# Attention with a maximum pass: the values matmuls of a full-width step in two halves, one unit of the maximum pass in between

## The reference, cut to what matters

```
q, k, v = heads(layernorm(x) @ W + b)            # 16 heads of 8
sim  = q @ k.T + bias(i - j) * SCALE             # relative position, bucketed
sim += where(j > i, -inf, 0)                     # causal
out  = softmax(sim) @ v                          # per head
x    = x + out @ Wo.T + bo
x    = x + layernorm(x + relu(t @ w1 + b1) @ w2 + b2) * gamma + beta    # t = layernorm(x)
```

## Time and profile before

| what | value |
|---|---|
| runs | 350.19, 349.46, 346.96 us; median 349.46 |
| the profiled execution | 348.02 us, its span 346.2 us |
| busy in the span | PE 291.8, DVE 273.9, ACT 189.5, POOL 86.9 us |
| one group, where the groups repeat (one to five) | 29.2 us |
| PE, DVE, ACT busy in it | 26.36, 25.90, 18.89 us |

### The profile page before, as it was taken

The page is one execution under the profiler, slowest core; times in us unless marked ns, Lnnn a source line. Parts: engine busy times, 40 slices in busy tenths (PEclk is TensorE's granted clock), DMA queues, the critical chain, the costliest instruction groups (busy, mean ns, idle before and its releaser), DMA issues.

```text
span 346.2 us, 8324 instructions
## 1 busy us (share of the span) xinstructions
PE 291.8 (84%) x3233; PEld 130.6 (38%) x3235; DVE 273.9 (79%) x968; ACT 189.5 (55%) x262; POOL 86.9 (25%) x127
## 2 busy tenths in 40 slices
PE   7855687878999998898999889889899888999980
PEld 4421332222334234334334423433433343358650
DVE  5565275688889888888989888898899968748895
ACT  2332198305656756765674685585566568762330
POOL 2114999700220202022022011202200001425351
PEclk9995599756999999999999999999999999999996
DMA  7445502540110112022020113123211102000022
GB/s 213 125 126 151 127 0 65 156 139 1 56 56 3 36 23 56 2 54 56 3 57 29 41 27 78 55 34 75 66 22 24 23 4 42 8 0 17 0 62 61
DMA packets 16263, 18.80 MB, mean 54 GB/s; under 512 B 4480, under 2 KB 11776, under 8 KB 16096
## 3 DMA queue, kind: packets, MB, share of 16 engines
q1 hardware_dynamic: 13488, 12.56, 15.3%
q10 hardware_dynamic: 816, 2.96, 3.0%
q0 software_dynamic: 1920, 2.76, 2.7%
HBM read 11.81 MB, written 4.23 MB: 46 GB/s over the span
## 4 chain that ended last, share of the span: by engine, by line
PE 51%; DVE 19%; ACT 14%; issue 6%; POOL 4%; DMA 3%; SPq 1%; ACTq 1%; DVEq 0%; POOLq 0%
PE ps L1145 16%; PE ps L1101 13%; ACT PT L729 9%; PE ps L1133 7%; PE ps L1116 7%; DVE FM L865 6%; DVE junk L872 3%; ACT TT L687 2%; POOL XN L566 2%; PE ps L1178 2%; PE ps L1034 2%; DVE st L929 2%; DVE U L982 1%; PE ps L1087 1%; DMA table_s<-in_table 1%
## 5 line engine op out<-in xcount | busy, mean ns | idle before, releaser
L729 ACT ACTIVATE PT<-ps 128x1024 f32<-128x1024 f32 (+1 forms) x192 | 144.7, 813 | 93.6 <-PE ps L1133 82.1
L865 DVE TENSOR_REDUCE FM<-ps 128x1 f32<-128x512 f32 (+2 forms) x192 | 109.2, 617 | 14.5 <-PE ps L1101 14.0
L872 DVE CUSTOM_DVE_ANT_0 junk<-ps,NBH 128x256 bf16<-128x256 f32 (+1 forms) x256 | 90.3, 400 | 24.7 <-PE ps L1101 24.5
L1101 PE MATMUL ps<-KA,QA 56*128 56x256 bf16 (+3 forms) x544 | 96.9, 292 | 10.6 <-DVE FM L865 7.4
L1116 PE MATMUL ps<-QA,KA 58*128 58x512 bf16 (+3 forms) x384 | 78.0, 334 | 17.5 <-ACT PT L729 14.6
L1145 PE MATMUL ps<-PT,VG 128*16 128x512 f32 (+3 forms) x768 | 87.3, 500 | 0.1
L1101 PEld LDWEIGHTS ps<-KA,QA 56*128 56x128 bf16 x544 | 33.0, 96 | 97.2 <-DVE FM L865 40.6
L420 POOL DMA_DIRECT2D KA<-qk_scratch x24 | 12.9, 542 | 156.7 <-PE ps L1133 156.4
L1116 PEld LDWEIGHTS ps<-QA,KA 58*128 58x128 bf16 x384 | 25.0, 94 | 37.1 <-ACT PT L729 30.2
L1133 PE MATMUL ps<-TT,flb 128*32 128x176 f16 (+4 forms) x1152 | 38.7, 244 | 0.0
L1133 PEld LDWEIGHTS ps<-TT,flb 128*32 128x32 bf16 x1152 | 21.5, 96 | 17.4 <-issue 15.8
(11 more groups left out here) (98 smaller groups left out, 261.1 us busy)
## 6 DMA issues: line engine op xcount, KB each, us to landing
QA<-qk_scratch SPq DMA_DIRECT2D x64, 48.0 KB
KA<-qk_scratch POOLq DMA_DIRECT2D x24, 96.0 KB, 2.7
qk_scratch<-QS SPq DMA_DIRECT2D x8, 192.0 KB
qk_scratch<-QS SPq DMA_DIRECT2D x12, 128.0 KB
X<-in_x SPq DMA_DIRECT2D x4, 256.0 KB, 5.5
PT<-fr_scratch ACTq DMA_DIRECT2D x1, 1024.0 KB, 4.7
out<-U SPq DMA_DIRECT2D x4, 256.0 KB, 2.3
OT<-f_scratch ACTq DMA_DIRECT2D x2, 480.0 KB, 6.4
```

What stands on the lines that cost most here:

```text
L729: nc.scalar.activation(PT[:, s % 3, 2 * q:2 * q + 2, off:off + w], ST[:, q, :, off:off + w], ACT.Exp).then_inc(s_exp, 1)
L865: nc.vector.tensor_reduce(FM[:, ib, heads[0]:heads[-1] + 1:2, piece], bank[:, 0:w * len(heads)].rearrange("p (h n) -> p h n", n=w), AX.X, ...
L872: last = nc.vector.tensor_tensor_reduce(junk[:, n % NSM, i, 0:w], bank[:, i * w:(i + 1) * w], nb[:, h, 256 - w:256], 1.0, NEG, ALU.add, AL ...
L1101: last = nc.tensor.matmul(SM[:, n % NSM, i * w + j - j0:i * w + j - j0 + nj], QA[r0:r0 + KS, p, ib // 4, q, (ib % 4) * 128:(ib % 4 + 1) * ...
```

## The change

`values` of a full-width step is issued in two halves of 256 columns, the four heads for columns 0 to 255 and then the four for 256 to 511. Between the halves `between()` issues the first unit of slot (s, 2), if that slot has one for this group; the rest of the slot follows the second half as before. Steps of 384 columns or fewer stay as they are. The semaphore for ScalarE (s_pv) is still raised by the last matmul of the step.

```diff
-            def values(g, p, s):
+            def values(g, p, s, between):
...
-                for h in range(HG):
-                    last = nc.tensor.matmul(OV[32 * h:32 * h + 2 * HD, off:off + w], VG[:, jb, g, h, :],
-                                            PT[:, s % 3, h, off:off + w], start=(jb == 0),
-                                            stop=(jb == 4 * ic + 3), skip_group_check=True)
+                cuts = [(off, w)] if w < IC else [(0, IC // 2), (IC // 2, IC // 2)]
+                for i, (c0, n) in enumerate(cuts):
+                    for h in range(HG):
+                        last = nc.tensor.matmul(OV[32 * h:32 * h + 2 * HD, c0:c0 + n], VG[:, jb, g, h, :],
+                                                PT[:, s % 3, h, c0:c0 + n], start=(jb == 0 and i == 0),
+                                                stop=(jb == 4 * ic + 3), skip_group_check=True)
+                    if i + 1 < len(cuts):
+                        between()
...
-                def s_units_at(s, pos):
-                    for later, k in (SLOTS0 if first else SLOTS).get((s, pos), []):
+                def s_units_at(s, pos, i0=0, i1=None):
+                    for later, k in (SLOTS0 if first else SLOTS).get((s, pos), [])[i0:i1]:
...
-                    values(g, p, s)
-                    s_units_at(s, 2)
+                    early = 1 if step_cols(*STEPS[s])[1] == IC else 0
+                    values(g, p, s, lambda: s_units_at(s, 2, 0, early))
+                    s_units_at(s, 2, early)
```

## The result

The changed kernel takes 346.78 us (median of 20 runs, 344.4 to 349.09), the kernel before 349.79 us (median of 20). The ratio is 0.9943, with a 95% interval of 0.9918 to 0.9969: about 2 us faster, 1.1 to 2.9. The ratio is taken over the fast runs of both kernels; a run of 397.68 us of the kernel before is not one of them (the other 19 lie between 345.66 and 351.56). The forecast was 347.0 us.

The account below looks back on a forecast made before the run. No engine had much room; short waits between TensorE, VectorE and ScalarE bounded it. Shifts of -0.44 and +0.08 gave -0.36 us a group, times seven -2.5 us: 349.46 to 347.0 us, range 343.3 to 353.

Parts of the forecast that it names:

- group 6: Seventh group with cuts, known to have more waits; taken to gain the same -0.36 us as the others.
- ScalarE's pair: Two exps of a step, 1.94 us; the next step's q = 1 scores cannot start before they end.
- unit 28's wait: Step 7: TensorE waited 0.41 us for VectorE to end unit 25; forecast to go, with ScalarE next.
- The price of a cut: Each full-width `values` cut with a unit in it: 0.18 us more of TensorE, turns of 0.10 us included.
- step 5: Cut around unit 18: unit 20 later, shift +0.14 us, for the biases and ScalarE's exps behind them.
- steps 6 and 7: Cuts around units 21 and 25: later q = 1 scores shifted -0.08 and -0.41 us, with ScalarE the next limit.
- step 8: Cut around unit 29: unit 33 starts at 184.85 instead of 185.29, shift -0.44 us.
- Step 0: Cut before the m transposes, which already cost a turn: +0.08 us, counted whole as TensorE waits for nothing there.
- A: Rival: turns at cuts cost twice 0.10 us, a cut 0.38 us; +0.64 us a group, 354 us; chance 0.2.
- B: Rival: VectorE sets the pace, ScalarE's limit is not reached; -0.85 us a group, 343.5 us; chance 0.15.
- D: Rival: half-clock stretches fall otherwise, worth up to about 8 us either way; chance 0.08, half each way.
- wait for its bank: Unit between halves: forecast never to wait, VectorE freeing its bank 0.4 us or more earlier; costed at nothing.

Follow-up runs that it names:

- e6: Changed kernel with only step 7 cut, unit 25 between the halves: group 28.82 us against 29.16 before, one run.
- e3: Changed kernel with cuts only at steps 0, 6, 7 and 8, one unit in each: group 28.50 us, ratio to before 0.9895.
- e4: Changed kernel cut at step 0 with one unit and at steps 6, 7, 8 with two units between halves: group 28.19 us, ratio to before 0.9816.
- e1: Changed kernel with all full-width steps in halves but no unit between: group 29.20 us, ratio to before 1.0003.
- e7: Changed kernel with only step 0 cut, one unit between the halves: group 29.08 us against 29.16 before, one run.
- e2: Changed kernel with only step 5 cut, unit 18 between the halves: group 29.40 us, ratio to before 1.0066.

## Why the prediction was right

**The frame.** A change of a few tenths in a group, from the difference of two larger things, was right: 347.0 forecast, 346.78 measured; a group of 28.8, measured 28.74. That the two totals lie 0.2 us apart is in part luck: the medians fell by 3.0 us, the ratio says 2.0, the forecast was 2.5, and it counted a gain for group 6 that did not come (below). The mechanism was right where it paid: step 7 alone is -0.34 (e6), ScalarE's pair was next, and unit 28's wait was gone.

**The price of a cut** was forecast at 0.18 us and is 0.23. A 256-column half that starts behind a unit takes 0.55 to 0.56 us; the `values` of the earlier trace rows starts behind the biases of a narrower step (0.53; 0.54 at the same place in e3 and e4). Why it is longer behind a unit isn't shown. The turn from the unit into `values` is 0.10 as read. At step 5 this makes 0.07 of the 0.10 us by which it came later than forecast (the units and scores behind the second half add the rest); steps 6 and 7 take that over through ScalarE's pair, less the 0.03 by which the scores now stand closer behind it, and step 8 adds its own 0.05. That the cost is in the turns was right (e1: halves alone +0.04 for six). By the Trainium skill, page TensorEngine Tiling (Array Packing), section Performance Considerations, the 48 added passes of e1 at 60 cycles each would be an estimated 1.2 us a group; the trace doesn't agree.

**Step 0** was mis-sized, +0.08 forecast against -0.09, in two ways. TensorE of after:

```profile
166.21 0.28 PE L1101 MATMUL ps<-KA,QA 56*128 56x128 bf16 x2
166.42 0.62 PE L1147 MATMUL ps<-PT,VG 128*16 128x256 f32 x8
166.87 0.39 PE L1087 MATMUL ps<-idb,MC 128*8 128x128 bf16 x4
```

The m transposes start 0.45 us behind the second half, where a unit needs 0.56: they pay no turn behind `values`, and come 0.03 us later against the start of the step than in before, not 0.08. And I looked for waits at the cuts only. Unit 3 is three places behind unit 1 and needs its bank. In before VectorE ends unit 1 at 165.31 and unit 3 starts at 165.37, 0.36 us behind the start of unit 2:

```profile
165.23 0.08 DVE L872 DVE_READ_ACCUMULATOR2_ANT FM<- 128x1 f32 x1
...
165.37 0.28 PE L1101 MATMUL ps<-KA,QA 56*128 56x256 bf16 x1
```

In after VectorE ends it at 167.04, ahead of unit 2 (167.18), and unit 3 starts 0.12 us or so behind unit 2, in the row at 167.30. I had taken that spacing of before for TensorE's own work. At the biases that follow, the shift against the start of the step is -0.09 (165.91 - 163.41 against 167.97 - 165.56), which is e7's -0.08 to -0.09.

**The rivals.** A (a turn at twice the price) was not so, but a quarter of the way to it was. B (VectorE sets the pace) fell for groups 1 to 5 with e2 and with ScalarE's pairs in the profile after; in group 6 VectorE does set the pace (below), without B's gain. D, the clock: in the two profiled executions after loses 3.0 us before group 1, where the granted clock differs, and this outweighs the gain of the groups; over 20 runs it did not. I haven't shown what places them.

**The sum over the kernel.** Five groups at -0.43 are -2.1 us. Group 6, from the copy of group 5's second block to that of its own, went from 30.59 to 30.69 us, +0.10, and group 7 from 29.49 to 29.51; from there to the end it is 36.1 us in both. That is -2.0 us, and the ratio gives -2.0 with 1.1 to 2.9. The prediction had -0.36 for each of seven groups, -2.5 us: too little for the five, and for group 6 ("I take the same for both") the wrong sign. What group 0 gained can't be read from two traces with another clock there.

In group 6 a unit between the halves does wait for its bank, which the prediction had costed at nothing and named as a sign of being wrong. VectorE has four reciprocals (L895) of 0.94 us there and in no other group. TensorE and VectorE of after at step 5 of group 6:

```profile
262.83 0.94 DVE L895 RECIPROCAL xnT<-xnT 128x128 f32<-128x128 f32 x1
...
263.30 0.63 PE L1147 MATMUL ps<-PT,VG 128*16 128x256 f32 x8
263.69 0.50 DVE L865 TENSOR_REDUCE FM<-ps 128x1 f32<-128x384 f32 x1
...
264.25 0.40 PE L1101 MATMUL ps<-KA,QA 56*128 56x128 bf16 x4 [0.32 <-DVE FM L865]
...
264.57 0.62 PE L1147 MATMUL ps<-PT,VG 128*16 128x256 f32 x8
```

Unit 18 needs the bank of unit 15, which VectorE frees at 264.19 (263.69 + 0.50); the unit starts 0.95 us behind the first half instead of 0.56, and the second half stands behind it. With step 5 alone cut (e2) group 6 lost 0.32 us, the others 0.24. And step 7 brings nothing there: in e6 group 6 is 30.59 us as in before, where the other groups gain 0.34. In after unit 27 starts at 270.85 there, 0.06 us behind VectorE's end of unit 24, whose bank it takes, and 0.50 us behind unit 26, its partner on the other half of the array. Without the cuts at steps 4 and 5 (e3) group 6 gains 0.23 us, the others 0.66. So what a cut is worth changed with the work that VectorE had of its own.

## What to carry to other kernels

When two engines hand work to each other through a few buffers, look in the trace for the consumer's idle time behind the producer's longest block and for the producer's wait a few units later; moving one unit ahead repairs both, up to the next engine's limit. Move as many units as have a free buffer at that place and no more (a second one at step 8 gained 0.3 us a group, a third one at steps 6 to 8 lost 0.6 us), look at the groups in which the other engine has more work, and pair what can run side by side. Judge each place alone: here one of six cuts lost as much as two thirds of what another gained, and leaving out the two that brought nothing or lost took the gain from 0.42 to 0.66 us a group. All of this is read from one kernel.

## What was not expected of the hardware

- Transposes with 8 output columns followed `values` with 16 almost without a gap (0.45 us behind the start of the half, stream 0.43), while a unit with 128 output columns needed 0.10 us more, and 0.10 again on the way back.
- Cutting four side-by-side float32 matmuls of 512 columns in two cost next to nothing here as long as the halves followed each other: +0.04 us for six in e1.
- The two halves of the array did not keep the order of the program between them. TensorE at step 5 of before: the scores of q = 0, which come behind all four matmuls of unit 18 in the program, start 10 ns after the first of these, on the other rows of the array, and ahead of the other three.

```profile
175.88 0.23 PE L1101 MATMUL ps<-KA,QA 56*128 56x128 bf16 x1
175.89 0.39 PE L1116 MATMUL ps<-QA,KA 58*128 58x512 bf16 x1
175.94 0.33 PE L1101 MATMUL ps<-KA,QA 56*128 56x128 bf16 x3
```
